# The first layer of block 0 ahead of the ranking of edges, and padding rows written by place instead of whole regions filled

## The chip, the cores and the metric

One core of one Trainium2 chip runs the whole program. The metric is the device time of one execution in microseconds (us), the median over several executions.

## The reference

Two graph layers over 512 nodes and 16,384 edges, all in float32, with a residual sum and a layer norm after each. Nearly all the work is the first layer's messages:

```python
m = gelu(h_E @ m0_w + m0_b)        # h_E: 16384 x 512, m0_w: 512 x 256
m = gelu(m @ m1_w + m1_b)          # 256 x 256
m = gelu(m @ m2_w + m2_b)          # 256 x 256
dh = segment_sum(m, src, 512) / 30
h = layer_norm(h_V + dh, ln1_g, ln1_b)
# then a three-matrix MLP over the 512 nodes and another layer norm
```

The second layer is attention over the heads of each node, `x1[dst] * x1[src]` summed over edges by `dst` (the kernel does this with a 512 x 512 matrix `count` of edges between nodes), a small MLP and a GRU cell.

## The kernel before

**Three-pass float32.** Every matmul of the messages is made from rounded operands and their remainders: ScalarE writes `x_hi` (rounded), VectorE writes `x_lo = x - x_hi`, TensorE adds three products. For the outputs of a layer, ScalarE evaluates the Gelu twice from PSUM (rounded `m_hi`, then `m_out`), and VectorE subtracts (`rest_0`, `rest_1`).

**Blocks.** The edges come in 32 blocks of 512. TensorE's order is written out: `layer_1(b)`, first half of `layer_0(b + 1)`, `layer_2(b)`, second half of `layer_0(b + 1)`, and from block 6 on `sum_sorted(b - 6)`. Each of the other engines has its own such order. On VectorE it is `rest_x(b + 2)`, `rest_1(b, 0)`, `rest_1(b, 1)`, `rest_0(b + 1, 0)`, `biased(b, 0)`, `biased(b, 1)` and last `rest_0(b + 1, 1)`, whose result TensorE's `layer_1(b + 1)` needs in its second half; from block 5 on, the preparing of a sorted chunk stands between these. On ScalarE it is the Gelus of layer 1, the first of layer 0 of the next block, `gelu_2(b)`, the second of layer 0, and `round_x(b + 3)`. `gelu_2(b)` writes the buffer `m2[b % 2]` and waits until the scatters of block b - 2, which read it, have landed (the semaphore `scattered`).

**Sorting.** To sum messages by source node with few products, the kernel sorts them by group of 128 source nodes. Blocks 0 to 29 make 8 sorts of 4 or 3 blocks. For each of 128 edges, GpSimd issues one indirect DMA (128 rows of 259 floats, 1,036 bytes each: a message, and three numbers of its edge) that scatters rows of `m2` into `sorted_rows` in HBM. Each group begins at a multiple of 128 rows, so up to 3 tiles' worth of rows (384) of each sort hold no edge; they must hold -1 in the number fields so that they match no node. The place of each row is worked out on the chip at the start: VectorE makes one-hot groups (`group_edges`), TensorE counts and ranks with 17 matmuls (`rank_edges`), VectorE turns ranks into row numbers (`place_edges`, which ends with the semaphore `placed`). GpSimd's loop waits for `placed` at block 0.

**The regions.** Before its scatters, the whole region of a sort (19 or 15 tiles of 128 rows) is filled with -1 by one DMA on SP's queue (`fill(s)`, L367, 2.46 or 1.94 MB), the first after the loads of x of blocks 1 and 2, the others in blocks 1, 5, 9 to 25. GpSimd waits for `filled[s]` at the first block of a sort.

**Reading back.** SP's `reload(q)` (L378) reads chunk q, 5 tiles or fewer, in block q + 4; for the first chunk of a sort it waits for the scatters of all its blocks. SP's queue is in order: x of block b + 3 (L362), the fill, and in block 26 `x_rows`, `d0_w` and `d1_w` (0.5, 1 and 4 MB), then the reload. VectorE takes chunk q in block q + 5 (`hot_dst`, L802, ahead of `rest_1(b, 1)`), ScalarE rounds it (L526), TensorE sums it in block q + 6. Chunks 0 to 29 are so spread over the blocks.

**The start.** TensorE does `rank_edges()`, 16 products of `ident` (`keep_warm`), then layer 0 of block 0. VectorE does `group_edges()`, the splits of the first weights and of x of block 0, then `place_edges()`.

## Time and profile before

| | |
|---|---|
| median of 3 runs | 637.98 us (633.39 to 640.4) |
| the profiled execution | 636.32 us, of which the span shown by the profile is 634.6 |
| TensorE matmul busy in the span | 595.0 us (94%) |
| VectorE, ScalarE, GpSimd busy | 459.5, 365.0, 189.2 us |
| HBM read, written | 66.69 MB, 35.53 MB |
| edge loop | until about 454 us |

Times are us from the span's start. PE is TensorE's matmuls, PEld its weight loads, DVE VectorE, ACT ScalarE, POOL GpSimd, SP the queue that issues most transfers. A float32 matmul in three passes is pipelined, so busy times of single matmuls overlap: 0.39 us each, but 0.23 us from start to start. "idle before <-X" is the time the engine stood still before an instruction and what ended that.

### The profile page before, as it was taken

What the parts mean: (1) busy time and instruction counts of PE and PEld (TensorE: products, weight loads), DVE (VectorE), ACT (ScalarE), POOL (GpSimd) and SP (SyncE); (2) the same over time, 40 slices, a digit from 0 to 9 for tenths busy, and PEclk for the clock granted to TensorE, in tenths of its full rate; (3) what the DMA queues carried; (4) which work ended last, traced back from release to release, by engine and by line L of the source; (5) the groups of instructions that cost most, each with busy time, mean ns of one, the idle gap of its engine ahead of it and who ended that gap; (6) DMA issues with size and microseconds to landing.
All of it is one profiled execution on the core that took longest, in us unless ns stands there. A gap on an engine that the chain in (4) does not pass through costs nothing.

```text
span 634.6 us, 9167 instructions
## 1 busy us (share of the span) xinstructions
PE 595.0 (94%) x3281; PEld 510.0 (80%) x3281; DVE 459.5 (72%) x777; ACT 365.0 (58%) x551; POOL 189.2 (30%) x179
## 2 busy tenths in 40 slices
PE   4999998999999999999999989987999999887994
PEld 2888887988898888888888878877988888676752
DVE  5746586777788878788877868798465466798646
ACT  4577686767776767776777756653183431211331
POOL 3044354345434554355534534400000001000100
PEclk9999999999999999999999989999899999999998
DMA  7994399397499479649639983331000514000000
GB/s 250 307 280 142 138 270 305 117 279 269 147 262 290 142 220 305 185 156 286 192 131 267 431 297 111 94 83 43 1 2 0 208 34 200 0 1 1 0 1 33
DMA packets 51483, 102.82 MB, mean 162 GB/s; under 512 B 3568, under 2 KB 41328, under 8 KB 46960
## 3 DMA queue, kind: packets, MB, share of 16 engines
q1 hardware_dynamic: 45104, 86.04, 44.1%
q0 software_dynamic: 5760, 15.92, 7.7%
q8 instruction: 28, 0.46, 0.3%
q10 hardware_dynamic: 576, 0.28, 0.2%
q14 instruction: 15, 0.12, 0.1%
HBM read 66.69 MB, written 35.53 MB: 161 GB/s over the span
## 4 chain that ended last, share of the span: by engine, by line
PE 78%; DMA 9%; DVE 7%; issue 2%; ACT 2%; POOL 1%; SPq 0%; POOLq 0%; DVEq 0%; ACTq 0%
PE ps L1191 24%; PE ps L1227 8%; DMA sorted_raw<-sorted_rows 7%; PE ps L1373 7%; PE ps L1233 4%; PE ps L1209 4%; PE ps L1205 4%; PE ps L1204 4%; PE ps L1341 3%; PE ps L1272 3%; PE ps L1276 3%; PE ps L1274 3%; PE ps L1384 2%; PE ps L1299 1%; PE ps L1411 1%
## 5 line engine op out<-in xcount | busy, mean ns | idle before, releaser
L452 POOL DMA_INDIRECT sorted_rows<-m,place x120 | 163.1, 1359 | 214.7 <-ACT m L514 186.2
L771 DVE TENSOR_TENSOR m_lo<-m_out,m_hi 128x512 fp32r<-128x512 f32 x128 | 88.8, 694 | 60.4 <-ACT m_out L499 57.0
L497 ACT ACTIVATE m_hi<-ps,cols 128x512 fp32r<-128x512 f32 x128 | 88.5, 691 | 75.5 <-PE ps L1191 47.5
L1191 PE MATMUL ps<-x_lo,w_hi 128*128 128x512 f32 x256 | 100.7, 393 | 0.0
L1191 PE MATMUL ps<-x_hi,w_hi 128*128 128x512 f32 x256 | 100.6, 393 | 0.0
L1191 PE MATMUL ps<-x_hi,w_lo 128*128 128x512 f32 x256 | 100.5, 392 | 0.0
L499 ACT ACTIVATE m_out<-ps,cols 128x512 f32<-128x512 f32 x128 | 88.1, 688 | 0.0
L687 DVE TENSOR_TENSOR x_lo<-x_raw,x_hi 128x1024 fp32r<-128x1024 f32 x64 | 75.7, 1223 | 7.4 <-ACT x_hi L491 7.4
L1227 PE MATMUL ps<-w_lo,m_hi 128*128 128x256 f32 x256 | 64.2, 283 | 0.0
L1227 PE MATMUL ps<-w_hi,m_hi 128*128 128x256 f32 x256 | 64.0, 282 | 0.0
L491 ACT ACTIVATE x_hi<-x_raw 128x1024 fp32r<-128x1024 f32 x62 | 62.3, 1059 | 1.8 <-DMA x_raw<-in_edges_dram 1.8
L514 ACT ACTIVATE m<-m_in 128x512 f32<-128x512 f32 x64 | 39.5, 634 | 40.3 <-DVE m_in L784 40.3
L802 DVE TENSOR_SCALAR pack_hot<-iota,sorted_raw 128x256 fp32r<-128x256 f16 x144 | 53.4, 407 | 7.7 <-DMA sorted_raw<-sorted_rows 7.7
L1191 PEld LDWEIGHTS ps<-x_hi,w_lo 128*128 128x128 f32 x256 | 48.5, 189 | 10.4
L1191 PEld LDWEIGHTS ps<-x_hi,w_hi 128*128 128x128 f32 x256 | 48.6, 190 | 9.4
L1191 PEld LDWEIGHTS ps<-x_lo,w_hi 128*128 128x128 f32 x256 | 48.5, 189 | 9.0
L784 DVE TENSOR_TENSOR m_in<-ps,m2b 128x512 f32<-128x512 f32 x64 | 41.2, 686 | 19.1 <-PE ps L1233 19.1
L1227 PEld LDWEIGHTS ps<-w_lo,m_hi 128*128 128x128 f32 x256 | 49.0, 191 | 1.2
L1205 PE MATMUL ps<-m_hi,w_lo 128*128 128x512 f32 x128 | 49.9, 390 | 0.0
L1204 PE MATMUL ps<-m_hi,w_hi 128*128 128x512 f32 x128 | 49.9, 390 | 0.0
L1227 PEld LDWEIGHTS ps<-w_hi,m_hi 128*128 128x128 f32 x256 | 48.9, 191 | 1.2
L1272 PE MATMUL ps<-sorted_hi,src_hot 128*128 128x256 f32 x144 | 42.9, 298 | 5.8 <-issue 3.8
(206 smaller groups left out, 1141.0 us busy)
## 6 DMA issues: line engine op xcount, KB each, us to landing
x_raw<-in_edges_dram SPq DMA_DIRECT2D x31, 1024.0 KB, 7.5
sorted_raw<-sorted_rows SPq DMA_DIRECT2D x24, 647.5 KB, 6.2
sorted_rows<-no_edge SPq DMA_DIRECT2D x6, 2460.5 KB, 19.3
d_w<-in_d_dram SPq DMA_DIRECT2D x1, 4096.0 KB, 26.6
sorted_rows<-no_edge SPq DMA_DIRECT2D x2, 1942.5 KB, 17.6
sorted_raw<-sorted_rows SPq DMA_DIRECT2D x6, 518.0 KB, 4.2
rows<-in_rows_dram SPq DMA_DIRECT2D x1, 2176.0 KB, 8.8
d_w<-in_d_dram SPq DMA_DIRECT2D x2, 1024.0 KB, 13.9
```

Of the source, the lines that this page charges most:

```text
L452: pool.indirect_dma_start(out=sorted_d, out_offset=bass.IndirectOffsetOnAxis(ap=place[:, at:at + 1], axis=0), in_=m2[:, b % 2, t], in_offs ...
L491: nc.scalar.activation(x_hi[:, b % 2, K_HALF[h]], x_raw[:, b % 2, K_HALF[h]], ACT.Copy).then_inc(x_hi_done, 1)
L497: nc.scalar.activation(out_hi[:, m], ps[:, bank], ACT.Gelu, bias=col(bias, m)).then_inc(hi_signal, 1)
L499: nc.scalar.activation(m_out[:, m], ps[:, bank], ACT.Gelu, bias=col(bias, m)).then_inc(signal, 1)
L687: nc.vector.tensor_tensor(x_lo[:, b % 2, ks], x_raw[:, b % 2, ks], x_hi[:, b % 2, ks].bitcast(F32), ALU.subtract).then_inc(x_lo_done, 1)
L771: nc.vector.tensor_tensor(lo[:, m], m_out[:, m], hi[:, m].bitcast(F32), ALU.subtract).then_inc(done, 1)
L802: nc.vector.tensor_scalar(pack_hot[:, q % 2, t], iota[:, 0:2 * P], near, unit, ALU.is_equal, ALU.mult)
L1191: last = nc.tensor.matmul(out, left, right, start=(k == 0 and i == 0), stop=(k == KE - 1 and i == 2))
L1204: nc.tensor.matmul(out, w(1, k, m, w_hi), m0_hi[:, k], start=(k == 0), stop=False, skip_group_check=True)
L1205: nc.tensor.matmul(out, w(1, k, m, w_lo), m0_hi[:, k], start=False, stop=False, skip_group_check=True)
L1227: nc.tensor.matmul(out, m1_hi[:, k, e], part[:, at:at + H], stop=False, skip_group_check=True, start=(k == 0 and part is w_hi and t % 2 == 0))
L1272: nc.tensor.matmul(group_sum[:, g], hot, sorted_hi[:, q % 2, t], start=False, stop=False, skip_group_check=True)
```

## The change

1. TensorE: `keep_warm` first (it now waits for `ident` itself), then both halves of layer 0 of block 0, and only then `rank_edges()`.
2. VectorE: the splits of the first weights and of the first half of x of block 0 come before `group_edges()`, the rest behind it. `place_edges` is cut in two: `count_groups()` runs in block 0 and `place_edges()` in block 1, both after `biased(b, 1)` and before `rest_0(b + 1, 1)`.
3. The eight fills and their waits go. A new function `pad_rows()` at the end of `place_edges` works out the row numbers of the 3 x 128 padding rows of each sort. GpSimd writes them from `no_edge` with 24 indirect DMAs, two in each of blocks 0 to 11, between the copy of the ids and the block's scatters.
4. SP waits for `padded[s]` before the first reload of a sort, and for all of them before `d1_w`, whose memory holds the row numbers.
5. GpSimd makes two more small iotas at the start.

```diff
@@ sync: load_x, fill and reload
-            def fill(s):
-                rows_s = sorted_d[s * TILES * P:(s * TILES + SORT_TILES[s]) * P].rearrange("(t p) f -> p t f", p=P)
-                all_rows = no_edge[:].rearrange("p (a f) -> p a f", a=1).to_broadcast([P, SORT_TILES[s], ROW])
-                sp.dma_start(rows_s, all_rows).then_inc(filled[s], 16)
-
...
                     for par in range(2):
                         sp.wait_ge(scattered[par], 64 * ((past + 1 - par) // 2))
+                    sp.wait_ge(padded[sort], 16 * PADS)
...
             load_x(1)
             load_x(2)
-            sp.wait_ge(consts, 1)
-            fill(0)
             for b in range(NBLK):
                 if b + 3 < NBLK:
                     load_x(b + 3)
-                if b % 4 == 1 and b // 4 + 1 < SORTS:
-                    fill(b // 4 + 1)
...
-                    sp.wait_ge(placed, 1)
+                    for s in range(SORTS):
+                        sp.wait_ge(padded[s], 16 * PADS)
                     sp.dma_start(d1_w[:].rearrange("p a b -> p (a b)"), d1_d).then_inc(early_loaded, 16)
@@ gpsimd: the loop over blocks
                 pool.tensor_copy(m2[:, b % 2, :, H:ROW], edge_id[:, b * TB:(b + 1) * TB]).then_inc(ids_in, 1)
-                if b in SORT_FIRST:
-                    pool.wait_ge(filled[SORT_FIRST.index(b)], 16)
+                for i in range(2 * b, min(2 * b + 2, PADS * SORTS)):
+                    rows_at = pad_place[:, i // PADS, i % PADS:i % PADS + 1]
+                    pool.indirect_dma_start(out=sorted_d, out_offset=bass.IndirectOffsetOnAxis(ap=rows_at, axis=0),
+                                            in_=no_edge[:], in_offset=None).then_inc(padded[i // PADS], 16)
                 pool.wait_ge(ids_in, b + 1)
@@ vector
+            def count_groups():
...
                 idx(nc.vector.tensor_reduce(group_n[:], totals, AX_X, ALU.add))
...
+                idx(nc.vector.tensor_tensor(tile_group[one], tile_past[one, 0], tile_past[one, 2], ALU.add))
+
+            def place_edges():
...
-                nc.vector.tensor_copy(place[:], place_f[:]).then_inc(placed, 1)
+                idx(nc.vector.tensor_copy(place[:], place_f[:]))
+                pad_rows()
+
+            def pad_rows():
+
+                idx(nc.vector.tensor_copy(before_n[:, 0], group_n[:, 0]))
+                idx_wait()
+                for g in range(1, PADS):
+                    idx(nc.vector.tensor_tensor(before_n[:, g], before_n[:, g - 1], group_n[:, g], ALU.add))
+                    idx_wait()
+                idx(nc.vector.scalar_tensor_tensor(before_n[:], group_at[:, 1:], float(P), before_n[:], ALU.mult, ALU.subtract))
+                idx_wait()
...
+                idx(nc.vector.tensor_tensor(pad_past[:], pad_no[:].to_broadcast(each), limit, ALU.is_ge))
...
+                idx_wait()
+                idx(nc.vector.tensor_tensor(pad_past[:], pad_past[:], rows_in, ALU.mult))
+                idx_wait()
+                idx(nc.vector.tensor_reduce(pad_n[:], pad_past[:].rearrange("p g s k -> p s k g"), AX_X, ALU.add))
+                idx_wait()
+                nc.vector.tensor_tensor(pad_place[:], pad_row[:], pad_n[:], ALU.add).then_inc(placed, 1)
...
+            rest_w(0)
+            rest_x(0, 0)
+            rest_w(1)
             group_edges()
-            for g in range(2):
-                rest_w(g)
-                rest_x(0, g)
+            rest_x(0, 1)
             rest_w(2)
             rest_w(3)
-            place_edges()
...
                 biased(b, 1)
+                if b < 2:
+                    (count_groups, place_edges)[b]()
@@ tensor
-            rank_edges()
+            pe.wait_ge(ident_ready, 1)
             keep_warm(16, 0)
             layer_0(0, 0)
             layer_0(0, 1)
+            rank_edges()
```

## Rows read from the trace of the kernel before

**Rows 1.** Windows by block: us, busy (xcount) by engine, PEclk, DMA share, GB/s
```profile
42.42:53.60 11.18, 11.18 (x63) 9.55 (x62) 6.33 (x9) 7.98 (x12) 4.62 (x5) 1.00 0.80 232
...
87.12:100.19 13.07, 11.39 (x62) 9.59 (x61) 8.91 (x13) 9.25 (x13) 6.20 (x5) 1.00 1.07 292
...
357.73:373.08 15.35, 13.14 (x77) 11.50 (x76) 9.98 (x16) 10.34 (x15) 6.30 (x5) 1.00 0.99 401
373.08:387.97 14.89, 14.89 (x78) 12.67 (x78) 12.04 (x20) 9.04 (x13) 6.53 (x5) 0.89 0.46 161
387.97:400.85 12.88, 12.88 (x77) 11.44 (x76) 10.54 (x17) 9.26 (x13) 6.39 (x5) 1.00 0.32 95
```

**Rows 2.** Timeline, start: time, us, engine line op, [idle before <-releaser]
```profile
3.35 0.29 POOL L432 TENSOR_SCALAR_AFFINE_SELECT ident<-ident 128x128 f32<-128x128 f32 x1
...
6.41 1.06 ACT L546 ACTIVATE x_hi<-x_raw 128x1024 fp32r<-128x1024 f32 x1 [1.74 <-DMA x_raw<-in_edges_dram]
...
13.62 3.73 PE L1299 MATMUL ps<-ident 128*128 128x128 f32 x32
...
16.04 1.28 ACT L497 ACT_TABLE_LOAD   x1
...
17.11 0.48 PE L1191 MATMUL ps<-x_hi,w_hi 128*128 128x512 f32 x1
...
22.66 0.39 PE L1204 MATMUL ps<-m_hi,w_hi 128*128 128x512 f32 x1
...
25.06 0.30 PEld L1209 LDWEIGHTS ps<-m_lo,w_hi 128*128 128x128 f32 x2 [0.39 <-DVE m_lo L771]
```

**Rows 3.** Timeline of the start, VectorE
```profile
6.59 0.23 DVE L710 TENSOR_SCALAR part_i<-src_i 128x128 int32<-128x128 int32 x1 [6.59 <-DMA dst_i<-in_dst_dram]
...
8.96 0.68 DVE L692 TENSOR_TENSOR w_lo<-w_raw,w_hi 128x512 fp32r<-128x512 f32 x1
...
9.56 1.22 DVE L687 TENSOR_TENSOR x_lo<-x_raw,x_hi 128x1024 fp32r<-128x1024 f32 x1
...
13.82 0.69 DVE L738 TENSOR_REDUCE group_n<-ps 128x32 f32<-128x512 f32 x1
...
16.82 0.67 DVE L759 TENSOR_TENSOR rank<-ps,group_row 128x512 f32<-128x512 f32 x1
...
19.58 0.23 DVE L766 CAST place<-place_f 128x128 int32<-128x128 f32 x1
```

**Rows 4.** Timeline of block 1, VectorE
```profile
46.66 0.69 DVE L771 TENSOR_TENSOR m_lo<-m_out,m_hi 128x512 fp32r<-128x512 f32 x1 [3.00 <-ACT m_out L499]
```

**Rows 5.** Timeline of block 2, ScalarE
```profile
54.28 1.24 ACT L514 ACTIVATE m<-m_in 128x512 f32<-128x512 f32 x2 [2.09 <-DVE m_in L784]
56.54 0.69 ACT L497 ACTIVATE m_hi<-ps,cols 128x512 fp32r<-128x512 f32 x1 [1.02 <-PE ps L1191]
```

**Rows 6.** Timeline of block 1, GpSimd
```profile
44.50 0.98 POOL L452 DMA_INDIRECT sorted_rows<-m,place  x1 [5.64 <-ACT m L514]
...
49.67 0.35 POOL L445 COPY m<-edge_id 128x12 f32<-128x12 f32 x1
```

**Rows 7.** The page's costliest groups: the scatters | busy, mean ns | idle before
```profile
L452 POOL DMA_INDIRECT sorted_rows<-m,place x120 | 163.1, 1359 | 214.7 <-ACT m L514 186.2
```

**Rows 8.** Time to landing of the scatters issued from 44 to 50 us
```profile
DMA to landing us min/median/max: 3.1/3.8/4.1
```

**Rows 9.** Timelines of blocks 6 and 27, VectorE, waiting for a reload
```profile
98.54 0.41 DVE L802 TENSOR_SCALAR pack_hot<-iota,sorted_raw 128x256 fp32r<-128x256 f16 x1 [3.28 <-DMA sorted_raw<-sorted_rows]
...
371.27 0.41 DVE L802 TENSOR_SCALAR pack_hot<-iota,sorted_raw 128x256 fp32r<-128x256 f16 x1 [4.45 <-DMA sorted_raw<-sorted_rows]
```

**Rows 10.** Timeline, SP's queue
```profile
76.54 0.43 SPq L367 DMA_DIRECT2D sorted_rows<-no_edge  x1
```

**Rows 11.** The page's DMA issues: count, KB each, median us to landing
```profile
sorted_raw<-sorted_rows SPq DMA_DIRECT2D x24, 647.5 KB, 6.2
sorted_rows<-no_edge SPq DMA_DIRECT2D x6, 2460.5 KB, 19.3
```

More of the change, by code:

```diff
@@ L49 @@
 NQ = len(CHUNKS)
+PADS = NC - 1
 COUNT_AFTER = (6, 13, 20, 26)
@@ L106, in gnn_kernel @@
         rank = sb("rank", [P, NC, SORTS, COLS_SORT])
+        pad_place = sb("pad_place", [P, SORTS, PADS], I32)
+        pad_no = sb("pad_no", [P, 1, SORTS, PADS])
+        pad_row = sb("pad_row", [P, SORTS, PADS])
+        pad_past = sb("pad_past", [P, PADS, SORTS, PADS])
+        pad_n = sb("pad_n", [P, SORTS, PADS])
+        before_n = sb("before_n", [P, PADS, SORTS])
         place_f = sb("place_f", [P, SORTS * COLS_SORT])
@@ L300, in gnn_kernel @@
         m2_biased, ids_in = sem("m2_biased"), sem("ids_in")
-        filled = [sem(f"filled{s}") for s in range(SORTS)]
+        padded = [sem(f"padded{s}") for s in range(SORTS)]
         scattered = [sem("scattered0"), sem("scattered1")]
@@ L435, in _ @@
                       allow_small_or_imprecise_dtypes=True)
+            pool.iota(pad_no[:], [[0, 1], [0, SORTS], [P, PADS]], base=0, channel_multiplier=1,
+                      allow_small_or_imprecise_dtypes=True)
+            pool.iota(pad_row[:], [[TILES * P, SORTS], [P, PADS]], base=0, channel_multiplier=1,
+                      allow_small_or_imprecise_dtypes=True)
             pool.iota(tile_no[:], [[0, SORTS], [CHUNK, TB], [1, CHUNK]], base=0, channel_multiplier=0,
@@ L757, in place_edges @@
                 idx(nc.vector.tensor_tensor(tile_past[one, 0], tile_past[one, 0], tile_past[one, 1], ALU.add))
+                idx_wait()
+                idx(nc.vector.tensor_tensor(tile_group[one], tile_past[one, 0], tile_past[one, 2], ALU.add))
+            def place_edges():
+                ranks = ps[:, CNT + 1].rearrange("p (g s c) -> p g s c", g=NC, s=SORTS)
                 first = group_row[:].rearrange("p g (s a) -> p g s a", a=1).to_broadcast([P, NC, SORTS, COLS_SORT])
@@ L760, in place_edges @@
                 idx_wait()
-                idx(nc.vector.tensor_tensor(tile_group[one], tile_past[one, 0], tile_past[one, 2], ALU.add))
                 idx(nc.vector.tensor_tensor(rank[:], rank[:], group_hot[:, :, :, COLS_SORT - 1:], ALU.mult))
@@ L765, in place_edges @@
                 idx_wait()
-                nc.vector.tensor_copy(place[:], place_f[:]).then_inc(placed, 1)
+                idx(nc.vector.tensor_copy(place[:], place_f[:]))
[8 more added lines that the diff above has]
+                idx_wait()
+                each = [P, PADS, SORTS, PADS]
+                limit = before_n[:].rearrange("p g (s a) -> p g s a", a=1).to_broadcast(each)
+                rows_in = group_n[:, 1:].rearrange("p g (s a) -> p g s a", a=1).to_broadcast(each)
+                idx(nc.vector.tensor_tensor(pad_past[:], pad_no[:].to_broadcast(each), limit, ALU.is_ge))
+                idx(nc.vector.tensor_tensor(pad_row[:], pad_row[:],
+                                            group_n[:, 0].rearrange("p (s a) -> p s a", a=1).to_broadcast([P, SORTS, PADS]),
+                                            ALU.add))
+                idx_wait()
+                idx(nc.vector.tensor_tensor(pad_past[:], pad_past[:], rows_in, ALU.mult))
+                idx_wait()
+                idx(nc.vector.tensor_reduce(pad_n[:], pad_past[:].rearrange("p g s k -> p s k g"), AX_X, ALU.add))
+                idx_wait()
+                nc.vector.tensor_tensor(pad_place[:], pad_row[:], pad_n[:], ALU.add).then_inc(placed, 1)
             def rest(hi, lo, signal, done, b, m):
@@ L1240, in rank_edges @@
                 pe.wait_ge(group_ready, 1)
-                pe.wait_ge(ident_ready, 1)
                 flat = group_hot[:].rearrange("p g s c -> p (g s) c")
```

2 lines of the change are left out of this document (removed).

## The prediction, made before the changed kernel ran

> **What bounds the kernel now.** I read the page's slices first, then the windows cut at block boundaries, then the timelines around the places where those windows differ. In the quiet blocks 1 to 5 a block takes 11.18 us and TensorE is busy for all of it; with a chunk of sorted edges in it, a block takes 12.88 us, again with TensorE busy throughout [rows 1]. VectorE, ScalarE and GpSimd have idle time in the same rows. So only a TensorE stall, or its removal, moves the end. There are three places to look at. The start: layer 1 of block 0 begins at 22.66 us, behind 17 ranking matmuls, 16 warming products and layer 0 [rows 2]. Block 6: 13.07 us where 11.18 would do. Blocks 27 and 28: 15.35 and 14.89 us where 12.88, and 12.88 plus 0.45 for clearing the count banks, would do [rows 1]. After the edge loop nothing that the change touches runs.
>
> **Start.** The change puts the split of the first half of x ahead of `group_edges`. That group of operations took 6.59 to 8.96 us, 2.4 us [rows 3]. ScalarE rounds the first half until 7.5 [rows 2]. The first half of `x_lo` then ends near 8.7, the weights' second half near 9.3, `group_edges` near 11.7, and the second half of `x_lo` near 12.9 (1.22 us for each half). TensorE warms on `ident`, ready at 3.6: 3.7 us for the 16 products, up to 7.5 if all at half clock, so done before 11.2 [rows 2]. Then 6 of layer 0's matmuls wait for the second half. From 12.9: 6 + 12 matmuls at 0.23 us (24 took 17.11 to 22.66) end at 17.05; ranking, 17 at the same 0.23 us, ends at 20.95. ScalarE has its Gelu table by 17.3 [rows 2], its first outputs are there before. Layer 1 so starts 1.7 us earlier, and the 0.4 us wait inside it at 25.06, which came from VectorE being busy with block 1's x behind the placing, goes. **Start: -2.1 us.** The bounds are -2.5 (ranking at the pace of its own bf16 operands, not of layer 0's) and -0.5 (half clock after the 2.5 us gap, rival D).
>
> **VectorE, blocks 0 and 1.** `count_groups` stood at 13.82 to 16.82 plus 0.3 for `tile_group`: 3.4 us. It now sits after `biased`, where VectorE idles 3.00 us before `rest_0(b+1, 1)` [rows 4]. That operation has no slack: layer 1 takes its result at once. **Block 0: +0.4 us.** Placing took 16.82 to 19.81, less 0.25 for the moved operation, 2.7 us. `pad_rows` is not in this trace: eight dependent small steps; one of 128x128 takes 0.23 us [rows 3], bounds 0.1 to 0.35 each; I take 0.22, 1.8 us, since they are smaller but each waits for the one before. Together 4.5 us in 3.0 us of cover. **Block 1: +1.5 us** (0.5 to 2.5). The cover is the first thing in those blocks; without it both cost their full 7.9 us.
>
> **GpSimd, blocks 0 to 3.** This is the new wait. `placed` came at 19.8 us and now comes at 43.66 + 4.5 - 2.1 + 0.4 = 46.5, when the scatter of block 0 is long due. Behind it on GpSimd's queue stand the copy of ids, two padding DMAs per block, then four scatters. Four took 44.50 to 49.67, 1.29 us each [rows 6]; over the whole kernel it is (163.1 + 214.7 - 186.2) / 120 = 1.60 us [rows 7]. With six on end, under all of VectorE's work, I take 1.35: nearer the early blocks, where they will run. Block 0's last scatter starts at 46.95 + 5 x 1.35 = 53.7 and lands 3.8 us later [rows 8], 57.5. ScalarE's Gelu of layer 2 of block 2 writes the buffer that this scatter reads. It ran at 54.28, now due at 54.1, and 1.02 us of slack follow it [rows 5]. Queued behind it are the second half's Gelu of layer 0 and x of block 5; VectorE's `rest_0(3, 1)` waits for the first, TensorE for that. **Block 2: 57.5 - 55.1 = +2.4 us.**
> The Trainium skill ("DMA: Bandwidth & Descriptors", Anatomy of one DMA) fits a GpSimd DMA as 2.0 us plus bytes over 436 GB/s, by our estimate 2.3 us for these 133 KB. By that block 2 would cost 0.9 us; the row's 3.1 to 4.1 us decides.
> Then the reload of the first sort. GpSimd now works without a pause: a block is 0.35 us for the copy [rows 6], 0.1 for waits and six DMAs of c us. Block 3's last scatter starts at 46.95 + 3 x (0.45 + 6c) + 5c = 48.3 + 23c, with c = 1.35 at 79.4, and lands by 83.4. SP waits for it, then issues the reload, and behind it on SP's queue x of block 8 and the second reload. A reload lands after 6.2 us in the median [rows 11], perhaps 4.5 with no fill beside it: 88.3. VectorE wanted the next one at 98.54 - 3.28 = 95.3 and TensorE lost 1.9 of those 3.28, so 1.4 are slack [rows 1, 9]. The first is wanted 11.2 earlier, plus a shift of 2.2, plus 1.4: 87.6. **Block 5: +0.7 us** (0 to 2.8). GpSimd catches up after that: 8.6 us of work in a block of 11.2. The padding DMAs of blocks 4 to 11 lie in its wait for the Gelu, which was 5.64 us at 44.50 against their 2.7 [rows 6], and cost nothing; in a block whose wait were gone they would cost those 2.7.
>
> **SP's queue.** Eight fills go, 2.46 MB and a median of 19.3 us to landing [rows 11]. One was issued at 76.54 just ahead of the second reload [rows 10], which landed at 98.5 while VectorE idled 3.28 us [rows 9]. Without it, that reload shares the queue with 1 MB and 0.65 MB and lands by 93 to 95, due at 97.7. **Block 6: -1.9 us.** The last fill, 1.94 MB, precedes the loads of x, `x_rows`, `d0_w` and the 4 MB `d1_w`, and the reload behind them landed at 371.27, 4.45 us late [rows 9]. Its 1.94 MB are worth 4.9 us at the 401 GB/s of block 27's window, 6.6 us at the 292 GB/s that block 6's window moved, with a fill in it, at the same full share of the DMA engines [rows 1]. The fill's short rows are in the second, so I take 6.6: more than the 4.45 late. TensorE then ran the next matmuls at half clock (0.89 over 14.89 us): that is the 1.6 us of block 28. **Blocks 27 and 28: 2.5 + 1.6 = -4.0 us** rounded. The waits for `padded` on SP are long met; `d1_w` waited for `placed`, now for the last padding DMA in block 11. GpSimd's two extra iotas lie under the index loads.
>
> **Sum.** -2.1 + 0.4 + 1.5 + 2.4 + 0.7 - 1.9 - 4.0 = -3.0 us. The profiled execution took 636.3 us (span 634.6), so 633.3; the median shown is 1.7 above it, so I forecast 635.0.
>
> **Rivals.**
> A. GpSimd is the bound of the early blocks (slower). Place: the six DMAs per block. Each 0.1 us more per DMA costs 2.3 us, so at 1.48 us the gain is gone. At the kernel's mean of 1.60, block 2 costs 3.6, block 5 5.2: +2.7, or 640.7; each of these stalls passes the 2.4 us after which row 373.08 shows the clock down, 1.6 us more each: 643.9. For it: the mean [rows 7]. Against: the early blocks' 1.29 [rows 6]. The Trainium skill ("GPSIMD Engine Reference", Specifications) says GpSimd shares its SBUF interfaces with VectorE's two-input operations; these are in the 1.29 already for half of the time.
> B. Scatters keep ahead: at 0.9 us per DMA, or a landing 2 us sooner, blocks 2 and 5 cost nothing: -6.1, 631.9. For it: without fills the writes have the engines alone. Against: the 3.8 us of block 1's scatters [rows 8].
> C. The 4 MB of `d1_w` alone hold the late reload, and the change does not do there what it removes: +4.0, 639.0. Against: 4.9 to 6.6 us saved are over 4.45.
> D. The gap in layer 0 near 10.3 to 12.9 us drops the clock as at 373.08: start only -0.5, 636.6. Against: a 1.9 us stall in block 6 left it at 1.00 [rows 1]; 2.5 did not.
>
> **Chances.** Forecast 0.50, A 0.18, B 0.14, C 0.08, D 0.10. Leaving out the far end of A and the sum of B's luck, the range is 629.5 to 642.5. About 1% is what a measurement can tell here: faster than 631.6 needs B with a good run, 0.19; slower than 644.4 needs A at its end, 0.12; within, 0.69. The likeliest case's own range is 632 to 638.
>
> **What would show it.** Right: layer 1 of block 0 near 21 us; ScalarE's Gelu of block 2 released by a scatter's landing near 57.5; no VectorE wait for a reload in blocks 6 and 27; both windows back to 11.2 and 12.9. Wrong: a GpSimd DMA above 1.48 us in blocks 0 to 3, TensorE windows of blocks 1 and 2 above 14 us, or a late reload near 366.

## The result, and the profile after

The changed kernel takes 651.62 us in the median of 4 executions (648.71 to 655.45); beside it the kernel before took 638.63. The ratio is 1.022, with a 95% interval of 1.018 to 1.026: it is slower, by about 2%. The forecast was 635.0, the range 629.5 to 642.5. The profiled execution took 653.4 us, its span is 651.6, 17.0 more than that of the profiled execution of before. (The medians are 13.0 apart. What follows adds up the 17.0 of the two profiles.)

| | before | after |
|---|---|---|
| span | 634.6 us | 651.6 us |
| TensorE matmul busy | 595.0 us | 601.1 us |
| GpSimd busy | 189.2 us | 216.6 us |
| HBM written | 35.53 MB | 19.62 MB |
| indirect DMAs | 120 | 144 |

The windows below are cut at the start of the second half of layer 0 in blocks 1 to 6, then blocks 27 and 28 (columns as in [rows 1]).

```profile
29.30:40.72 11.42, 11.36 (x63) 9.56 (x61) 9.30 (x22) 7.98 (x12) 0.00 (x0) 1.00 0.23 82
40.72:53.31 12.59, 11.35 (x62) 9.55 (x61) 10.31 (x22) 8.08 (x12) 5.66 (x5) 1.00 0.27 73
53.31:68.41 15.10, 12.94 (x63) 10.75 (x62) 6.42 (x8) 7.89 (x12) 12.04 (x14) 0.89 0.51 181
68.41:90.87 22.46, 14.89 (x62) 12.02 (x61) 6.46 (x9) 7.97 (x12) 11.95 (x14) 0.85 0.55 186
90.87:102.02 11.15, 11.15 (x63) 9.56 (x61) 7.60 (x12) 9.14 (x13) 7.26 (x7) 1.00 0.39 115
102.02:113.20 11.18, 11.18 (x63) 9.56 (x61) 9.97 (x16) 9.14 (x13) 7.72 (x7) 1.00 0.71 210
370.58:383.46 12.88, 12.88 (x78) 11.44 (x76) 11.13 (x18) 10.23 (x15) 6.29 (x5) 1.00 1.03 363
383.46:396.76 13.30, 13.30 (x80) 11.54 (x78) 11.07 (x18) 9.04 (x13) 5.94 (x5) 1.00 0.32 100
```

Against the same windows of before the difference adds up so:

| place | after | before | change | forecast |
|---|---|---|---|---|
| to the second half of layer 0 of block 1 (start) | 29.30 | 31.24 | -1.9 | -2.1 |
| next window (count_groups) | 11.42 | 11.17 | +0.2 | +0.4 |
| next (place_edges, pad_rows) | 12.59 | 11.18 | +1.4 | +1.5 |
| 53.31 to 68.41 (Gelu of block 2) | 15.10 | 11.18 | +3.9 | +2.4 |
| 68.41 to 90.87 | 22.46 | 11.18 | **+11.3** | 0 |
| the reload of block 6 | 11.18 | 13.09 | -1.9 | -1.9 (and +0.7) |
| blocks 27 and 28 | 26.17 | 30.23 | -4.1 | -4.0 |
| behind the start of the second half of layer 0 of block 31 (one more stretch at half clock, 435 to 439 us) | | | +1.7 | 0 |
| GpSimd's last instruction | | | **+6.4** | 0 |

Five of the steps came out as forecast within 0.2 us. Two things that the prediction never named cost 17.7 us together. The first is in these rows, with the releaser where the trace gives one. A signal is here the update of a semaphore by which one engine tells another that an instruction is over. (The trace of after lacks some records of semaphores, so it says "issue" or "remote" in places.)

```profile
46.54 0.59 POOL L449 COPY m<-edge_id 128x12 f32<-128x12 f32 x1 [39.90 <-DVE pad_place L800]
55.04 0.96 POOL L458 DMA_INDIRECT sorted_rows<-m,place  x1 [0.30 <-issue]
57.97 1.15 ACT L520 ACTIVATE m<-m_in 128x512 f32<-128x512 f32 x2 [6.06 <-DMA sorted_rows<-m,place]
59.74 0.79 PE L1240 MATMUL ps<-m_hi,w_hi 128*128 128x512 f32 x1 [2.16 <-ACT m_hi L503]
...
67.92 0.64 PE L1269 MATMUL ps<-w_hi,m_lo 128*128 128x256 f32 x4
69.89 1.29 DVE L818 TENSOR_TENSOR m_in<-ps,m2b 128x512 f32<-128x512 f32 x2 [2.17 <-PE ps L1269]
70.93 0.39 PE L1227 MATMUL ps<-x_hi,w_lo 128*128 128x512 f32 x1
76.34 0.69 ACT L503 ACTIVATE m_hi<-ps,cols 128x512 fp32r<-128x512 f32 x1 [4.50 <-remote]
77.08 0.80 PE L1240 MATMUL ps<-m_hi,w_hi 128*128 128x512 f32 x1 [4.19 <-issue]
78.96 1.05 PE L1245 MATMUL ps<-m_lo,w_hi 128*128 128x512 f32 x2
85.55 0.69 ACT L503 ACTIVATE m_hi<-ps,cols 128x512 fp32r<-128x512 f32 x1 [6.05 <-remote]
86.29 0.39 PE L1263 MATMUL ps<-w_hi,m_hi 128*128 128x256 f32 x1 [3.38 <-ACT m_hi L503]
```

The first four rows are the forecast chain: `placed` at 46.5 (forecast 46.5), block 0's last scatter at 55.04 (forecast 53.7), ScalarE's Gelu of block 2 at 57.97 (forecast 57.5), TensorE's wait behind it. The rest is new. The last matmul of layer 0's second half (L1227) ends at 71.3. ScalarE's Gelu waits for that matmul alone, stands idle, and starts at 76.34. The two of L1245 end by 80.0, and the Gelu that waits for the first of them starts at 85.55. VectorE's L818 starts 1.3 us after its matmul. The records of the semaphores agree: the update by the matmul of 71.31 is at 76.32, those of the two L1245 at 85.53 and 85.56. In the kernel before the Gelu at 56.54 [rows 5] starts 0.03 us after its matmul, and from 20 to 400 us no update comes over 0.15 us late. Meanwhile only GpSimd works, an indirect DMA every 1.27 us and none of its waits over 0.31 us from 46.5 to 83.4. TensorE's two idle stretches, 4.2 and 3.4 us, and the half clock behind each (0.85 over the window, 3.4 us) make 11.0 of the 11.3.

The second is at the very end. The last instructions of the two kernels, from the trace's own records (start, duration):

```
before  GpSimd DRAIN 630.76 1.48   SyncE DRAIN 634.34   end 634.56
after   GpSimd DRAIN 641.43 9.97   SyncE DRAIN 645.01   end 651.63
```

DRAIN is the instruction that closes an engine's program. GpSimd's begins with its last operation (a power, for the layer norm) in both. In the kernel before it is over at 632.24, ahead of SyncE's, which comes when the output has landed. In the changed kernel it ends at 651.40, 6.4 us behind SyncE's.

### The profile page after: what moved, and what is told of

It reads as the page before. It is cut to its first block, busy times and chain, and to the rows that moved or that the text cites. A ratio compares the mean times of both kernels' runs of the same rounds, so it can differ in the third digit from the quotient of the medians.

```text
span 651.6 us, 9204 instructions
## 1 busy us (share of the span) xinstructions
PE 601.1 (92%) x3281; PEld 515.6 (79%) x3281; DVE 461.6 (71%) x786; ACT 365.0 (56%) x551; POOL 216.6 (33%) x205
## 3 DMA queue, kind: packets, MB, share of 16 engines
HBM read 66.69 MB, written 19.62 MB: 132 GB/s over the span
## 4 chain that ended last, share of the span: by engine, by line
PE 80%; DVE 8%; issue 4%; ACT 3%; another core or an unknown queue 2%; DMA 1%; POOL 0%; POOLq 0%; DVEq 0%; SPq 0%; ACTq 0%
PE ps L1227 25%; PE ps L1263 9%; PE ps L1409 7%; PE ps L1269 4%; PE ps L1245 4%; PE ps L1240 4%; PE ps L1241 4%; PE ps L1377 3%; PE ps L1307 3%; PE ps L1311 3%; PE ps L1309 3%; PE ps L1420 2%; PE ps L1447 1%; PE ps L1495 1%
## 5 line engine op out<-in xcount | busy, mean ns | idle before, releaser
L1227 PE MATMUL ps<-x_hi,w_hi 128*128 128x512 f32 x256 | 100.7, 393 | 1.6 <-DVE x_lo L693 1.6
L1227 PE MATMUL ps<-x_lo,w_hi 128*128 128x512 f32 x256 | 100.1, 391 | 0.0
L1227 PE MATMUL ps<-x_hi,w_lo 128*128 128x512 f32 x256 | 99.8, 390 | 0.0
L818 DVE TENSOR_TENSOR m_in<-ps,m2b 128x512 f32<-128x512 f32 x64 | 41.2, 686 | 23.4 <-PE ps L1269 23.4
L1227 PEld LDWEIGHTS ps<-x_hi,w_hi 128*128 128x128 f32 x256 | 48.5, 189 | 11.3 <-DVE x_lo L693 2.0
L1240 PE MATMUL ps<-m_hi,w_hi 128*128 128x512 f32 x128 | 51.5, 402 | 6.4 <-issue 4.2
L1227 PEld LDWEIGHTS ps<-x_hi,w_lo 128*128 128x128 f32 x256 | 48.2, 188 | 10.4
L1227 PEld LDWEIGHTS ps<-x_lo,w_hi 128*128 128x128 f32 x256 | 48.5, 189 | 8.9
L467 POOL TENSOR_TENSOR rstd<-var_eps,minus_half 128x2 f32<-128x2 f32 (+1 forms) x11 | 8.0, 732 | 125.6 <-DVE var_eps L955 125.6
```

The source lines that it names most:

```text
L1227: last = nc.tensor.matmul(out, left, right, start=(k == 0 and i == 0), stop=(k == KE - 1 and i == 2))
L1240: nc.tensor.matmul(out, w(1, k, m, w_hi), m0_hi[:, k], start=(k == 0), stop=False, skip_group_check=True)
```

## The experiments

One table for all; times beside the kernel before on the same chip, with the 95% interval of the ratio in brackets. The columns from "block 8" on are of one profiled execution each. "Block 8" and "block 31" are the starts of the second half of layer 0 in those blocks. "DMAs" is the count of indirect DMAs, "DRAIN" the length of GpSimd's last one.

| kernel | median us | before | ratio | block 8 | block 31 | DMAs | DRAIN |
|---|---|---|---|---|---|---|---|
| before (profile above) | 637.98 | | | 113.93 | 413.20 | 120 | 1.48 |
| after (profile above) | 651.62 | 638.63 | 1.022 | 126.94 | 422.14 | 144 | 9.97 |
| e1_move_only | 636.22 | 636.18 | 1.000 (0.997-1.003) | 112.51 | 412.26 | 120 | 1.48 |
| e2_pads_only | 638.35 | 636.18 | 1.004 (1.001-1.006) | 112.52 | 407.73 | 144 | 9.97 |
| e3_one_per_block | 639.95 | 636.18 | 1.006 (1.003-1.009) | 113.31 | 408.52 | 144 | 8.91 |
| e4_extra_dmas | 641.91 | 636.18 | 1.008 (1.005-1.011) | 112.65 | 414.00 | 144 | 7.03 |
| a1_again | 650.2 | 635.38 | 1.022 (1.018-1.026) | 125.67 | 420.87 | 144 | 9.97 |
| g1_split_fills | 644.33 | 635.38 | 1.014 (1.010-1.017) | 117.98 | 419.76 | 120 | 1.48 |
| d1_132_dmas | 642.62 (one) | 635.38 | | 113.92 | 415.45 | 132 | 7.68 |
| a2_third | 646.63 | 635.93 | 1.016 (1.011-1.021) | 120.47 | 415.67 | 144 | 9.97 |
| e3_again | 639.17 | 635.93 | 1.005 (1.002-1.009) | 113.56 | 408.77 | 144 | 8.91 |
| i1_late_dummies | 651.29 | 635.93 | 1.023 (1.018-1.028) | 122.00 | 420.77 | 128 | 9.64 |
| h1_two_sorts | 637.48 | 635.93 | 1.002 (1.000-1.004) | 113.60 | 408.81 | 126 | 8.91 |
| k2_late_memsets | 646.28 | 636.39 | 1.016 (1.008-1.025) | 121.10 | 417.38 | 120 | 1.48 |
| k9_dummies_behind | 649.13 | 636.39 | 1.021 (1.016-1.026) | 121.19 | 420.39 | 128 | 9.32 |
| k5_120_two_kinds | 633.83 (one) | 636.39 | | 112.82 | 412.26 | 120 | 1.48 |
| h2_last_sort | 639.74 | 636.39 | 1.005 (1.001-1.008) | 116.55 | 411.75 | 123 | 8.67 |
| m1_moved_fills | 632.18 | 636.19 | **0.994 (0.991-0.997)** | 112.91 | 408.12 | 120 | 1.48 |
| m2_moved_fills_order | 637.16 | 636.19 | 1.001 (0.998-1.004) | 117.42 | 412.62 | 120 | 1.48 |
| k3_memsets_12 | 643.89 | 636.28 | 1.012 (1.008-1.016) | 121.06 | 418.55 | 120 | 1.48 |

### The two halves of the change, and the pace of its DMAs

The new order alone (from the kernel before; the part on VectorE is shown):

```diff
-            group_edges()
-            for g in range(2):
-                rest_w(g)
-                rest_x(0, g)
+            rest_w(0)
+            rest_x(0, 0)
+            rest_w(1)
+            group_edges()
+            rest_x(0, 1)
...
-            place_edges()
...
+                if b < 2:
+                    (count_groups, place_edges)[b]()
```

> The kernel before with the new order alone: layer 0 of block 0 first, count_groups in block 0, place_edges in block 1; the fills stay and nothing is padded, so 120 indirect DMAs. The changed kernel lost 11.3 us in block 5's window, where TensorE's signals to ScalarE came 4 to 6 us late while GpSimd issued DMAs without a pause from 46.5 to 83.4 us, and 8.5 us in GpSimd's last DRAIN (9.97 us where it was 1.48). Theory 1 (a long unbroken run of indirect DMAs delays the signals): here the run is 16 DMAs in four blocks of some 5.5 us, from about 45 to 67 us, half as long, so no or little stall: block 5's window within 1 us of 11.2, start -1.9, block 0 +0.3, and the two fills' losses kept: 1.7 us under before. Rival 1 (the late placing itself upsets the early blocks): block 5 keeps most of its 11.3 us, some 10 us over before. Theory 2 (the long DRAIN comes with the number of indirect DMAs, 144 against 120): DRAIN 1.5 us here.

No stall: rival 1 falls. Block 8 starts 1.4 us sooner than in the profile of before, but the window of 51.9 to 64.6 is 12.69, since ScalarE's Gelu of block 2 waits 4.83 us for block 0's scatter even without padding. In all the time is that of before. Of the 1.9 us won at the start, 1.5 are given back there. (Most of the 1.4 us at block 8 is not the order's. e4 and k5 below have the old order and the code of the kernel before up to there, and are at block 8 at 112.65 and 112.82.)

The padding alone (the changed kernel with ranking and placing back at the start, `pad_rows` behind it):

> The other half alone: only the 384 padding rows written, with two indirect DMAs in each of blocks 0 to 11 and no fills, but ranking and placing at the start as before (with pad_rows behind it). GpSimd has its pauses in every block. Theory 1: no late signals, no stall in blocks 1 to 5; block 6 -1.9 us and blocks 27 and 28 -4.0 as in the changed kernel; the start +1.9 for pad_rows ahead of VectorE's first operation for layer 1. Compute so ends 4 us earlier than before. Rival 1 (the padding DMAs as such, writes to rows beside those of the scatters, make the signals late): a stall of several us shows here too. Theory 2 (DRAIN by the count of indirect DMAs, 144 here): 10 us DRAIN, and so 8.5 less 4.0, some 2 to 4.5 us over before in time. Rival 2 (the DRAIN goes with something the late order did, such as the unbroken stretch): DRAIN 1.5 us, 4 us under before.

No stall either, and the edge loop ends 5.5 us earlier. DRAIN is 9.97, and the time is 2.2 us over before. The step from fills to padding brought what it was meant to, and the last DRAIN took more than all of it.

The changed kernel with one padding DMA per block:

```diff
-                for i in range(2 * b, min(2 * b + 2, PADS * SORTS)):
+                for i in range(max(b - 1, 0), min(b, PADS * SORTS)):
```

> The changed kernel with one padding DMA in each of blocks 1 to 24 in place of two in each of blocks 0 to 11. GpSimd's work in a block falls from 8.0 to 6.7 us, so the unbroken stretch ends at about 75 us in place of 93 and holds some 20 DMAs in place of 36. Block 0's last scatter starts 2.5 us sooner, so ScalarE's Gelu of block 2 is not held: block 2's part of 3.9 us goes. Theory 1: block 5's 11.3 us go wholly or mostly: 15 us under the changed kernel, or 637 with the long DRAIN. Rival 1 (the late order or the missing fills make the stall, whatever GpSimd's pace): block 5 keeps over 5 us, time over 642. Theory 2: 144 indirect DMAs as in the changed kernel, so DRAIN 10 us.

Its windows of blocks 4 and 5:

```profile
53.32:66.06 12.74, 11.64 (x63) 9.49 (x62) 6.34 (x9) 7.78 (x12) 10.29 (x12) 1.00 0.49 170
66.06:77.22 11.16, 11.16 (x63) 9.56 (x62) 6.33 (x9) 7.97 (x12) 8.50 (x10) 1.00 0.44 165
```

The 11.3 us are gone, with the same order, no fills and 144 DMAs: 0.6% over before in place of 2.2%. That leaves the pace in the early blocks, by which GpSimd is also less late. Is a long unbroken run of such DMAs enough? Here is one in the old order:

```diff
+                for i in (range(6) if b in (8, 9, 10, 11) else ()):
+                    at = (b - 8) * 6 + i
+                    pool.indirect_dma_start(out=scratch_d, out_offset=...(ap=place[:, at:at + 1], axis=0),
+                                            in_=no_edge[:], in_offset=None).then_inc(extra, 16)
```

> The kernel before with 24 indirect DMAs added, six more ahead of the scatters in each of blocks 8 to 11, which write rows of no_edge to a tensor that nobody reads. GpSimd then has 10 x 1.27 + 0.35 = 13 us of work in blocks of 11.2 and runs without a pause from about 120 to 170 us. Theory 1: TensorE's signals come 4 to 6 us late somewhere in that stretch, TensorE idles for them, and the windows of blocks 9 to 13 together grow by over 5 us. Rival 1 (the stall of the changed kernel had another cause): those windows grow only by the lateness of the scatters, 4 x 1.9 us less the 5 us by which a buffer has time, 2 to 4 us, each stall released by a DMA's landing and not by TensorE. Theory 2: 144 indirect DMAs, so the last DRAIN is 10 us; rival 2: 1.5 us.

GpSimd issued from 114.7 to 186 us with no pause over 0.75 us, and every signal in this profile was on time. One window grew by 1.5 us. The DRAIN was long.

That does not settle it. d1_132_dmas (below, at the DRAIN) has the same six extra DMAs in blocks 8 and 9 only, and its profile does have late signals:

```profile
154.57 1.29 DVE L790 TENSOR_TENSOR m_in<-ps,m2b 128x512 f32<-128x512 f32 x2 [2.20 <-remote]
...
173.24 0.69 ACT L503 ACTIVATE m_hi<-ps,cols 128x512 fp32r<-128x512 f32 x1 [2.06 <-PE ps L1215]
```

The matmul that VectorE waits for had ended at 152.10 and its signal came at 154.55; the one ScalarE waits for had ended at 172.27 and its signal came at 173.21. TensorE did not stop for the first: that window is 12.86 us, as before. The second's is 12.86 too; the window behind it grew by 1.5 us, with 1.22 us of idle time at 182.06, which may come from it. So neither the new order nor the early blocks are needed for a late signal. An unbroken run of indirect DMAs brought them in d1 and not in e4, and theory 1 is neither shown nor refuted by e4 alone.

### Does it come back, and does it need the padding?

The changed kernel again, twice:

> The changed kernel once more, unchanged, for a second profile and more times. Four runs of its relatives have spoken against the first theory: 40 indirect DMAs on end in the kernel before (blocks 8 to 11) and 20 in the changed kernel with one padding DMA per block left every TensorE signal on time. So either the stall of block 5 (22.5 us where 11.2 would do, signals 4 to 6 us late) belongs to two padding DMAs per block in this place and is there each time (theory 1): block 5 above 20 us again, median near 651. Or it is an accident of that execution (rival 1): the windows after block 2 are 11.2, 12.6, 12.7 to 15.1, then 11.2, and the time is 640 to 645: 636.3 - 1.9 + 0.2 + 1.4 + 1.5 to 3.9 - 1.9 - 4.1 and 6.4 for the DRAIN. Theory 2 (DRAIN by the count of DMAs): 9 to 10 us again.

> The changed kernel a third time, for comparison with the three kernels of this call on the same chip. Its block 5 took 22.5 and 21.1 us in the two profiles so far. Theory 1 (the place and pace of the padding DMAs): again above 20. Rival (something of that chip): this profile may show 11.2, and then e3_again shows which kernels do it on this chip.

The first has the same stall, 21.1 us in the same window. In the second blocks 4 and 5 took 14.1 and 12.3 us, with a late signal further on, still inside GpSimd's unbroken stretch (here to 115.4). The two matmuls of L1245 end by 113.7, the Gelu that waits for the first starts at 116.4:

```profile
116.40 0.69 ACT L503 ACTIVATE m_hi<-ps,cols 128x512 fp32r<-128x512 f32 x1 [4.94 <-remote]
117.70 0.69 DVE L805 TENSOR_TENSOR m_lo<-m_out,m_hi 128x512 fp32r<-128x512 f32 x1 [4.79 <-ACT m_out L505]
```

So the size and the place vary from execution to execution. The three medians of this kernel are 1.6 to 2.2% over before.

> One padding DMA per block (blocks 1 to 24) in place of two, a second time. Theory 1: blocks 4 and 5 at 12.7 and 11.2 us as in its first profile, 640 in all, 10 us under the changed kernel on this chip. Rival: a stall like the changed kernel's where that one has it too.

No late signal on the same chip, and 639.2 us, 7.5 less than a2 beside it.

With the fills kept, nothing padded, and two unused indirect DMAs ahead of the scatters in blocks 0 to 3:

```diff
+                for i in (range(2) if b < 4 else ()):
+                    at = 2 * b + i
+                    pool.indirect_dma_start(out=scratch_d, ..., in_=no_edge[:], in_offset=None).then_inc(extra, 16)
```

> The new order alone with the fills, and two more indirect DMAs ahead of the scatters in each of blocks 0 to 3, which write unused rows to a tensor of their own: GpSimd has the changed kernel's six DMAs per block in the same place, from 44.6 to about 80 us, but nothing is padded and 128 DMAs are issued in all. Theory 1a (it is GpSimd's pace there: six DMAs per block, more than a block late): the same stall, blocks 4 and 5 together above 30 us where they take 23.9 without the extra DMAs. Theory 1b (it needs the padding's own writes, or the missing fills): 24 to 28 us, the scatter's lateness alone. The last DRAIN: 1.5 us if the step lies above 128 DMAs, 7 to 10 us if at or below.

```profile
52.36:65.83 13.47, 11.68 (x63) 9.48 (x62) 6.29 (x8) 7.77 (x12) 10.71 (x13) 1.00 0.54 178
65.83:85.93 20.10, 13.47 (x63) 11.08 (x62) 6.55 (x9) 7.99 (x12) 9.68 (x12) 0.83 0.44 143
...
73.21 0.69 DVE L794 TENSOR_TENSOR m_in<-ps,m2b 128x512 f32<-128x512 f32 x1 [8.01 <-remote]
75.37 0.80 PE L1216 MATMUL ps<-m_hi,w_hi 128*128 128x512 f32 x1 [6.63 <-DVE m_in L794]
```

The stall is back: 33.6 us in blocks 4 and 5, where the order alone took 23.9. Here it is VectorE that gets TensorE's signals late: those of the matmuls of 65.75 and 65.99 come at 73.19 and 74.60, 7.4 and 8.6 us behind. Neither the padding's own writes nor the missing fills are needed.

The same two DMAs behind the scatters of their block:

> As i1 (new order, fills, two extra indirect DMAs in each of blocks 0 to 3), but the two extra ones come behind the four scatters of their block. The pace and the unbroken stretch of GpSimd are the same; each block's scatters start 2.5 us sooner, so ScalarE's Gelu of block 2 waits only 1.5 us as in the move alone and block 3's about 2 us less. Theory A (pace of the DMAs while GpSimd is behind): stall again, blocks 4 and 5 together 28 to 34 us. Theory C (ScalarE's wait for the late scatter is needed for it): 24 to 26 us.

```profile
81.96 1.29 DVE L794 TENSOR_TENSOR m_in<-ps,m2b 128x512 f32<-128x512 f32 x2 [4.56 <-remote]
83.30 0.50 PE L1216 MATMUL ps<-m_hi,w_hi 128*128 128x512 f32 x1 [2.74 <-DVE m_in L794]
```

Blocks 4 and 5 took 24.1 us, as theory C wanted, but the late signal came one block on (matmuls over at 77.8, signals at 81.9), long after ScalarE's wait for a scatter. It does not need that wait; the expectation was right on the two blocks and wrong on what it stood for.

Last, GpSimd as late as in i1 but with memsets in place of the extra DMAs, in blocks 0 to 3 and then in blocks 0 to 11:

```diff
+                for i in (range(2) if b < 4 else ()):      # k3: b < 12
+                    pool.wait_ge(count_step, 1)
+                    wait(pool, busy, 2 * b + i)
+                    pool.memset(count[:, 0:3], 0.0).then_inc(busy, 1)
```

> The new order alone with the fills, and in each of blocks 0 to 3 two more memsets of GpSimd (128x1536, on the count that is zero anyway, 1.3 us each by the 1.80 us of 128x2048 at 4.29) ahead of the scatters, where the kernel i1 had two more indirect DMAs. GpSimd is as late and as unbroken as there, with four DMAs per block in place of six. Theory A (the signals of TensorE come late by the indirect DMAs' pace, six in a block while GpSimd is behind): no stall; blocks 4 and 5 together 24 to 27 us, only the scatter's lateness. Theory B (it is GpSimd's lateness, by the chain of scatters and ScalarE alone): 30 us or more as in i1 (33.6).

> As k2 (new order, fills kept, 120 indirect DMAs), with the two extra memsets in each of blocks 0 to 11, where the changed kernel has its two padding DMAs: GpSimd is as late and as long unbroken as there (some 8.3 us of work in a block of 11.2 to 12.9). Theory A (late signals of TensorE need the extra DMAs): none; blocks 4 and 5 near 26.1 as in k2, each loss released by a DMA's landing. Theory B (GpSimd's lateness is enough, whatever it works on): VectorE or ScalarE waits of 3 to 7 us for a matmul long ended, as in i1 and in the changed kernel, somewhere from 60 to 120 us. If there is none here either, five profiles of six DMAs per block with late signals stand against two of memsets without.

In k3 GpSimd never waits over 0.31 us from 44.8 to 100.5 us. Its ScalarE waits from 50 to 105 us that are longer than in a quiet block:

```profile
55.81 1.15 ACT L518 ACTIVATE m<-m_in 128x512 f32<-128x512 f32 x2 [5.24 <-DMA sorted_rows<-m,place]
67.85 1.16 ACT L518 ACTIVATE m<-m_in 128x512 f32<-128x512 f32 x2 [4.17 <-DMA sorted_rows<-m,place]
104.13 1.28 ACT L530 ACTIVATE sorted_hi<-sorted_raw 128x1280 fp32r<-128x1280 f32 x1 [5.53 <-DMA sorted_raw<-sorted_rows]
```

Each is ended by a transfer. No signal of TensorE is late in the profiles of k2 and k3. Both are 8.6 us behind e1 by block 8 all the same: to late scatters, behind those to the third sort's fill that the late reload now meets (VectorE waits 4.88 and 7.49 us for it), and in k2 1.9 of them to half clock at the start. i1 and k9 are 9.5 and 8.7 behind e1 there, 1.6 of k9's by the same half clock. So a late GpSimd costs about the same with late signals and without. What i1 and k9 take over k2 and k3 in all, 3 to 7 us, is about what their longer DRAIN adds to the span (6.1 and 5.7).

So late signals are in 5 of 5 profiles with six DMAs per block while GpSimd is behind (after, a1, a2, i1, k9) and in d1, and in none of 2 with four DMAs and memsets. That points to the DMAs; it does not prove it, for three reasons. e4 had the DMAs and no late signal. k2 was executed twice, and the profile is of the quick one (642.05 us; the other took 650.51). And the traces differ in kind: 12 of the 20 lack some updates of semaphores, and all six with late signals are among these. The eight that have every update (before, e1, e2, e3_one_per_block, e4, k3, m1, m2) have none that is late. e3_again, k2, g1, h1, h2 and k5 lack some and have none late either. Whether the tracing itself has a part in it, no run here tells. The loss of time is in each of the ten executions of the changed kernel: 645.25 to 655.45 us.

The Trainium skill ("Perfetto Trace Analysis", Tensor Engine Instruction) says that the end of a matmul in a profile is computed, and that TensorE gives its signal only when PSUM has acknowledged the writes. By that either the writes or the signal could be what is held up. No run here tells which: the next matmuls of TensorE, from 71.24 on, start on time, and the trace shows no writes to PSUM.

### What makes the last DRAIN long?

> The kernel before with 12 extra indirect DMAs of unused rows (six in each of blocks 8 and 9) in place of 24: 132 in all. The last DRAIN was 1.5 us with 120 and 7.0 to 10.0 with 144. If it grows with the count over 120, 3.5 to 5.5 us here; if there is a step between 120 and 144 (128, say), either 1.5 or the full 7 and more.

It fits the step; the length is not in proportion, since 132 gave 7.68 and 144 between 7.03 and 9.97.

The last block's four scatters replaced by unused rows to another tensor, 120 in all (those 512 edges are left out of the sum):

```diff
+                    unused = b == DIRECT[0] - 1
+                    pool.indirect_dma_start(out=scratch_d if unused else sorted_d, ...,
+                                            in_=no_edge[:] if unused else m2[:, b % 2, t], ...)
```

> The kernel before with 120 indirect DMAs as ever, but the last block's four write rows of no_edge to a tensor of their own in place of its edges, so 512 edges are left out of the sum. Theory count (the last DRAIN is long once more than 120 and at most 126 DMAs were issued): DRAIN 1.5 us. Theory kind (it is long when indirect DMAs of two kinds, another source and target, were issued): 7 to 10 us.

1.48 us. It is the count and not the kind. All eight kernels with 120 DMAs have 1.48; 123 is long already (h2, below). Somewhere from 121 to 123 the DRAIN becomes 7 to 10 us.

### Versions meant to be faster

Padding only for the third and the last sort, whose fills were the two that a reload collided with (126 DMAs), and only for the last (123):

> A version meant to be faster: ranking and placing at the start as before, fills as before but for the two that a reload collided with (the third and the last sort), whose 384 padding rows are written by three indirect DMAs each, one per block in blocks 4 to 9. 126 indirect DMAs. If the two collisions are what the fills cost, block 6 gains 1.9 us and blocks 27 and 28 4.0, less 0.5 for pad_rows: 5.4 under before, near 631 with a DRAIN of 1.5 us. If the step of the DRAIN lies at 126 or lower, 6 us more: 637. Rival (the next fill collides in their place): less gained.

> A version meant to be faster: as the two-sort version, but only the last sort's fill (1.94 MB, the one that held the reload behind d1_w) is replaced by three padding DMAs; 123 indirect DMAs in all. Blocks 27 and 28 give 4.0 us and pad_rows takes 0.5. With a short DRAIN: 3.5 under before, 632.5. With the long one (5.3 us more of span, if one padding DMA is enough to bring it): 638. Count theory leaves either open (the step lies between 120 and 126), kind theory says long.

h1's edge loop ends 4.4 us earlier, and the DRAIN of 8.91 takes 5.3 of span. In h2 the third sort's fill stays, and its reload stood in VectorE's way for 3.67 us, with half clock behind.

Fills in four parts, one per block behind the reload, in the new order:

> A version meant to be faster: the new order alone (layer 0 of block 0 ahead of the ranking, placing in block 1), the fills kept but each split into four parts of 0.6 MB, one per block behind the reload, the last in block 24. 120 indirect DMAs, so the short DRAIN. If the fills only cost what they collide with (theory): start -1.9 and +0.3 as in the move alone, block 6 -1.9 or so, blocks 27 and 28 -4.0: some 7 us under before, 629. Rival (the fills' bytes and short rows cost wherever they stand): each block's window grows by a late x or reload, and nothing or less than 3 us is gained.

The rival holds. Blocks 27 and 28 gain 4.1 us, but six windows grow by 0.8 to 4.5 us over those of e1. ScalarE's Gelu of block 2 waited 8.39 us for block 0's scatter, beside 4.83 in e1.

Two fills issued two blocks sooner, nothing else:

```diff
+FILL_AT = (1, 3, 9, 13, 17, 21, 23)
...
-                if b % 4 == 1 and b // 4 + 1 < SORTS:
-                    fill(b // 4 + 1)
+                if b in FILL_AT:
+                    fill(FILL_AT.index(b) + 1)
```

> The kernel before with two fills issued two blocks sooner and nothing else: the third sort's in block 3 in place of 5 (so it is over before the two reloads issued at 75 to 77 us), the last sort's in block 23 in place of 25 (before x_rows, d0_w and d1_w). 120 indirect DMAs, so the short DRAIN. Theory (what the fills cost is these two collisions): block 6's window 11.2 for 13.1 and blocks 27 and 28 12.9 and 13.3 for 15.3 and 14.9: 5.9 us under before, 630.3. Rival (a fill's bytes cost wherever it goes, as with the split fills): another window grows by as much.

> The same two fills moved, with the new order (layer 0 of block 0 first, count_groups and place_edges in blocks 0 and 1). The order alone brought 1.4 us to block 6 and 0.9 to the end of the edge loop in its profile, -1.9 at the start and 0.2 and 1.5 lost to counting and to block 0's late scatter. So 1.4 us under m1, 629, if nothing new collides; the third sort's fill now runs beside the late scatters of blocks 0 and 1 (45 to 70 us) and could hold one back: then 1 to 4 us more.

m1's windows of blocks 6, 27 and 28, to be held against [rows 1]:

```profile
88.00:99.20 11.20, 11.20 (x63) 9.57 (x62) 9.99 (x16) 9.14 (x13) 6.20 (x5) 1.00 0.62 183
356.56:369.43 12.87, 12.87 (x78) 11.43 (x76) 11.13 (x18) 10.22 (x15) 6.30 (x5) 1.00 0.97 341
369.43:382.73 13.30, 13.30 (x80) 11.54 (x78) 11.06 (x18) 9.03 (x13) 5.90 (x5) 1.00 0.33 101
```

All three waits are gone with the bytes still written and 120 DMAs. 632.18 us against 636.19, a ratio of 0.994 (0.991 to 0.997): the fastest version here, from a table of seven numbers.

Why 4.0 us and not the 5.9 of the windows? The loss in block 6 is not the same each time. k5 runs the code of the kernel before up to its last blocks, and has 11.26 us in that window, with the fill issued in the same place:

```profile
87.85:99.11 11.26, 11.26 (x62) 9.62 (x61) 8.92 (x13) 9.14 (x13) 6.20 (x5) 1.00 1.08 289
```

e4 has 11.17 and d1 12.05 there, against 13.09 in the profile of before. Blocks 27 and 28 together took 30.2 to 31.0 us in all four.

In the new order (m2) the third sort's fill, issued at 48.70, runs beside the late scatter of block 0; ScalarE waits 8.01 us for it and TensorE 4.12, with half clock behind: 18.3 us for that block, and the gain is gone.

## Why the prediction was wrong

- **Start, count_groups, placing:** right. Layer 1 of block 0 began at 20.76 (forecast 20.95), block 1's placing cost 1.4. For the start there was luck in this execution: rival D, half clock behind the gap in layer 0, did not come in its profile (1.56 us idle before 12.78), but it is real. In a2, the same kernel, TensorE stood still 2.42 us before 13.60, the clock fell, and the second half of layer 0 of block 1 began at 31.74 in place of 29.30. (The first row below is of PE alone.) It fell there in 4 of the 12 profiles with the new order (a2, g1, k2, k9), behind 2.23 to 2.43 us of idle time; in the others, with 1.05 to 2.18, it stayed up.

```profile
14.00:17.00 3.00, 3.00 (x8) 0.50 0.82 262
13.60 0.61 PE L1227 MATMUL ps<-x_hi,w_hi 128*128 128x512 f32 x1 [2.42 <-DVE x_lo L693]
```

- **GpSimd's pace, block 2:** the chain was right, and its end to half a microsecond by luck. Block 0's DMAs came every 1.54 us in the mean, so its last scatter was issued at 55.04, 1.3 us later than forecast; but ScalarE started 2.9 us behind that, and not the 3.8 taken from [rows 8]. Later DMAs came every 1.27 us for the most part, and block 3's last scatter was issued at 79.48, forecast 79.4. TensorE stood still 2.16 us of the forecast 2.4. Missed were the 1.7 us of half clock behind it (0.89 over the window). The prediction had them only in rival A, where it took 2.4 us of idle time as the point after which the clock falls. The runs show no such point: in block 2's window 1.61 us idle was followed by half clock in k2 (0.89), 2.31 us was not in a2 (1.00).
- **Block 5:** this is the step that failed. The prediction asked of an unbroken GpSimd only when its own results are late, and found slack. It took for granted that the signals between the other engines keep their time, and put this term at nothing. They came up to 5.9 us late, and the block cost 11.3 us more. e1, e2 and e3 show that it takes the late placing together with the two extra DMAs per block, and i1 that it takes neither the padding's writes nor the missing fills. Nothing in the trace of before could show it: no such stretch is in it. (With memsets in place of the extra DMAs, in kernels that keep the fills, a late GpSimd cost as much by block 8 with no late signal: k2, k3. So the slack that the prediction saw was not there either way.) Why the signals come late stays open.
- **Reload of the first sort (+0.7):** not tested in the changed kernel, where the blocks had slipped by 15 us. The reload was issued at 82.46 (forecast 83.4).
- **Fills:** right in size against the profile of before, and in cause. m1 shows the same 5.9 us in those windows with the fills merely moved, so it was collision, as [rows 9 to 11] were read. Block 6's 1.9 us were priced from one execution, though, and three others of the same code lost 0 to 0.9 there; the 4.0 us of blocks 27 and 28 come each time. The prediction did not ask whether moving a fill would do.
- **The end:** "after the edge loop nothing that the change touches runs" was wrong. 24 more indirect DMAs bring a DRAIN of 9.97 us in place of 1.48. The sum lacked 6.4 us for that. With k5 and h2 it is shown to go by the count, with a step from 121 to 123; why, is open.
- **Rival A** had the right sign for a reason that did not occur: over blocks 0 to 3 c was 1.34 in the mean, near the 1.35 of the forecast and not above 1.48. B and C fall with the rows above.
- **The scatter's landing:** 2.9 us after its issue, as said, less than the 3.1 to 4.1 of [rows 8]. The Trainium skill's fit ("DMA: Bandwidth & Descriptors", Anatomy of one DMA), by our estimate 2.3 us for 133 KB, is nearer to this one than it was to the rows of before.

What stays open: what holds TensorE's signals back, why ten DMAs per block did it in d1 and not in e4, whether the tracing has a part in it, and what the DRAIN does for 7 to 10 us.

## What to carry to other kernels

When a large transfer costs time only where it meets another, move it before removing it: two fills issued two blocks sooner gave 4 us, where 24 small DMAs in place of all fills (e2) cost 2. Price a wait from more than one execution: block 6's was 1.9 us in one and near nothing in two others. Work that is put on GpSimd's queue is to be counted over the whole program, since its last DRAIN lies on the end of the kernel, and a GpSimd that falls a block behind costs more than its own lateness. Try a change of two independent parts in parts: each half here was within 0.4% of before, the whole was 2.2% slower.

## What the hardware showed that was not expected

- TensorE's signals reached ScalarE or VectorE 1.3 to 8.6 us after the matmul's end while GpSimd was behind and issued six indirect DMAs of 133 KB per block of 11.2 us (after, a1, a2, i1, k9), and up to 2.4 us after it with ten per block in d1; within 0.15 us in the kernel before and in e4. Size and place differ between executions of one kernel, and only traces that lack some updates show it.
- GpSimd's last DRAIN: 1.48 us with 120 indirect DMAs, 8.67 with 123, 8.91 with 126, 7.03 to 9.97 with 128 to 144.
- The granted clock fell to 1.2 GHz after TensorE had stood still for 1.61 us in one kernel (k2) and stayed at 2.4 GHz after 2.31 us in another (a2). A fall cost 1.7 us in the changed kernel's block 2 (0.89 over 15.10 us) and 3.4 in i1 (0.83 over 20.10 us).
